# Signs-and-sizes output for one batch half only, whole output weights for the other, and new engine orders

## The reference, cut to what matters

```python
def _tower(x, w_in, b_in, blocks):
    h = _leaky(x @ w_in + b_in)
    for w1, b1, w2, b2 in blocks:
        h = _leaky(_leaky(h @ w1 + b1) @ w2 + b2 + h)
    return h

def step(prev_delta, xk):
    fk, k = xk
    d = where(k == 0, fk[:, 3], prev_delta)
    fk = fk.at[:, 3].set(d)
    fe = _tower(fk[:, :4], fw_in, fb_in, flat_blocks)      # depends on the step before
    pe = _tower(fk[:, 4:], pw_in, pb_in, path_blocks)      # does not
    h = _leaky(concatenate([fe, pe], -1) @ cw1 + cb1)
    delta = sigmoid(h @ cw2 + cb2)[:, 0]
    return delta, delta
```

## Time and profile before

| | us |
|---|---|
| median of 3 runs | 1308.1 (1307.48 to 1308.73) |
| the profiled execution's own time | 1308.0 |
| its span | 1306.2 |
| PE busy | 1284.5 (98%) |
| PE weight loads | 1049.5 (80%) |
| ACT busy | 996.0 (76%) |
| DVE busy | 866.4 (66%) |
| POOL busy | 23.2 (2%) |

### The profile page before, as it was taken

The page is one execution under the profiler, slowest core; times in us unless marked ns, Lnnn a source line. Parts: engine busy times, 40 slices in busy tenths (PEclk is TensorE's granted clock), DMA queues, the critical chain, the costliest instruction groups (busy, mean ns, idle before and its releaser), DMA issues.

```text
span 1306.2 us, 20302 instructions
## 1 busy us (share of the span) xinstructions
PE 1284.5 (98%) x6020; PEld 1049.5 (80%) x6020; DVE 866.4 (66%) x1801; ACT 996.0 (76%) x2177; POOL 23.2 (2%) x19
## 2 busy tenths in 40 slices
PE   5999999999999999999999999999999999999998
PEld 3788888888888888888888888888888888888885
DVE  4676666666666666666766666666676666666665
ACT  1677877777787777777778777777777777777786
POOL 6000000000000000000000000000000000000000
PEclk9999999999999999999999999999999999999999
DMA  4400000000000000000000000000000000000000
GB/s 151 190 10 9 11 11 9 9 12 10 9 11 11 9 11 10 10 9 11 11 9 11 11 9 10 11 10 9 11 10 10 11 10 10 10 11 10 9 7 2
DMA packets 14033, 23.53 MB, mean 18 GB/s; under 512 B 6324, under 2 KB 6760, under 8 KB 13160
## 3 DMA queue, kind: packets, MB, share of 16 engines
q1 hardware_dynamic: 13640, 22.23, 5.4%
q10 hardware_dynamic: 288, 0.01, 0.0%
HBM read 15.66 MB, written 6.55 MB: 17 GB/s over the span
## 4 chain that ended last, share of the span: by engine, by line
PE 97%; DVE 1%; ACT 1%; DMA 1%; issue 0%; SPq 0%; DVEq 0%; ACTq 0%
PE ps_path L438 34%; PE ps_res L441 19%; PE ps_flat L438 17%; PE ps_head L528 8%; PE ps_head L533 8%; PE ps_head L541 4%; PE ps_path L453 2%; PE ps_head L546 2%; PE ps_flat L497 2%; DVE p_res L347 1%; DMA x_lo<-chunk_lo 0%; ACT head L244 0%; DMA chunk_x<-x 0%; ACT head_hi L244 0%; DVE p_sum L350 0%
## 5 line engine op out<-in xcount | busy, mean ns | idle before, releaser
L244 ACT ACTIVATE f_mid<-ps_flat,columns_sb 128x256 f32<-128x256 f32 x512 | 243.0, 475 | 190.3 <-PE ps_flat L438 184.0
L441 PE MATMUL ps_res<-f_mid,hidden_w 128*128 128x256 f32 x1024 | 318.6, 393 | 0.5
L438 PE MATMUL ps_path<-p_mid,hidden_w 128*128 128x256 f32 x1024 | 306.4, 382 | 0.8 <-ACT p_mid L244 0.8
L244 ACT ACTIVATE f_res<-ps_res 128x256 f32<-128x256 f32 x512 | 196.1, 383 | 62.9 <-PE ps_res L441 62.6
L350 DVE SCALAR_TENSOR_TENSOR p_sum<-ps_path,columns_sb,p_res 128x512 f32<-128x512 f32 x128 | 96.0, 750 | 223.0 <-PE ps_path L438 223.0
L441 PEld LDWEIGHTS ps_res<-f_mid,hidden_w 128*128 128x128 f32 x1024 | 164.3, 188 | 82.6 <-ACT f_mid L244 43.2
L438 PEld LDWEIGHTS ps_path<-p_mid,hidden_w 128*128 128x128 f32 x1024 | 196.0, 192 | 28.6 <-ACT p_mid L244 1.5
L407 DVE TENSOR_SCALAR ps_res<-f_res,columns_sb 128x256 f32<-128x256 f32 x256 | 123.6, 483 | 121.0 <-ACT f_res L244 121.0
L347 DVE SCALAR_TENSOR_TENSOR p_res<-p_sum 128x512 f32<-128x512 f32 x256 | 182.3, 712 | 0.1
L244 ACT ACTIVATE p_mid<-ps_path,columns_sb 128x512 f32<-128x512 f32 x256 | 175.1, 684 | 7.7 <-PE ps_path L438 7.7
L528 PE MATMUL ps_head<-p_res,hidden_w 128*128 128x256 f32 x512 | 153.5, 382 | 3.8 <-DVE p_res L347 3.8
(11 more groups left out here) (39 smaller groups left out, 1390.0 us busy)
## 6 DMA issues: line engine op xcount, KB each, us to landing
x_path<-x_hi SPq DMA_DIRECT2D x256, 16.0 KB
x_path<-x_lo SPq DMA_DIRECT2D x256, 16.0 KB
x_flat<-x_hi SPq DMA_DIRECT2D x256, 6.0 KB
x_flat<-x_lo SPq DMA_DIRECT2D x256, 6.0 KB
chunk_x<-x SPq DMA_DIRECT2D x2, 1152.0 KB, 7.2
x_hi<-chunk_hi SPq DMA_DIRECT2D x2, 1152.0 KB, 8.8
x_lo<-chunk_lo SPq DMA_DIRECT2D x2, 1152.0 KB, 11.4
out<-delta SPq DMA_DIRECT2D x128, 2.0 KB
```

The costliest lines, as they stand in the source:

```text
L244: return act.activation(dst, src, ACT.Prelu, bias=bias, scale=scale, alpha=NEG)
L438: return pe.matmul(dst, weight[w_name], src, start=True, stop=True)
L441: return pe.matmul(dst, weight[w_name], src, start=False, stop=True, skip_group_check=True)
```

## The change

1. Group 0 keeps the signs and the two one-pass products. Its sizes now sit in its combine weights: `cw1_scaled` holds cw1 with each column multiplied by |c|, made once at the start. ScalarE then needs no scale for `head`, only the scaled bias. `head_hi` is no longer a second activation, but a copy of `head` to fp32r on VectorE.
2. Group 1 drops signs, sizes, `head_hi` and `head_lo`. Its head is the plain leaky with cb1, and one fp32 matmul with `cw2_rep`, the output weights repeated over 128 columns, makes the output (`output`).
3. The leaky of `path_2b` (p_res2) moves from VectorE to ScalarE.
4. The lists of the three engines are new: group 1 runs half a step apart from group 0, and its `flat_1a` and `flat_1b` of the next step stand at the end of a body.
5. At the start come one more small DMA (cw2 as a row), a small matmul that spreads that row over the partitions, and four VectorE steps that make `cw2_rep`, `cw2_sizes` and `cw1_scaled`. PE now waits for five of these parts instead of two.

```diff
+            cw2_at = COLUMNS.index("cw2")
+            act.dma_start(cw2_row[:, :], w["columns"][:, cw2_at:cw2_at + 1].rearrange("p a -> a p"),
+                          allow_slow_non_contiguous=True)\
+               .then_inc(s_columns, 16)
...
-            def leaky(dst, src, bias=0.0, scale=1.0):
-                return act.activation(dst, src, ACT.Prelu, bias=bias, scale=scale, alpha=NEG)
+            def leaky(dst, src, bias=0.0):
+                return act.activation(dst, src, ACT.Prelu, bias=bias, alpha=NEG)
...
+            def path_2b(k):
+                par = k % 2
+                if exists(k):
+                    act.wait_ge(s_p2b_t, k + 1)
+                    leaky(p_res2[par][:, :], p_sum2[:, :]).then_inc(s_p2b_h, 1)
...
-                    leaky(head[g][:, :], combined(g), cb1_scaled[:, :], cw2_size[:, :]).then_inc(s_head_h[g], 1)
-
-            def head_high(k, g):
-                if exists(k):
-                    act.wait_ge(s_head_mm[g], k + 1)
-                    leaky(head_hi[g][:, :], combined(g), cb1_scaled[:, :], cw2_size[:, :]).then_inc(s_head_hi[g], 1)
+                    leaky(head[g][:, :], combined(g), cb1_scaled[:, :] if g == SPLIT else column["cb1"]).then_inc(s_head_h[g], 1)
...
+            dve.tensor_copy(cw2_rep[:, :], column["cw2"].to_broadcast([HID, HID])).then_inc(s_cw2, 1)
+            dve.wait_ge(s_cw2_rows, 1)
+
+            dve.tensor_copy(cw2_copy[:, :], cw2_rows).then_inc(s_cw2_parts, 1)
+            dve.wait_ge(s_cw2_parts, 3)
+            dve.scalar_tensor_tensor(cw2_sizes[:, :], cw2_copy[:, :], -1.0, cw2_copy[:, :],
+                                     ALU.mult, ALU.max).then_inc(s_cw2_parts, 1)
+            dve.wait_ge(s_cw2_parts, 4)
+            dve.wait_ge(s_w_loaded, 16)
+            for i, n in enumerate(("cw1_flat", "cw1_path")):
+                dve.tensor_tensor(cw1_scaled[:, i * HID:(i + 1) * HID], weight[n], cw2_sizes[:, :],
+                                  ALU.mult).then_inc(s_cw2, 1)
...
+            def head_high(k, g):
+                if exists(k):
+                    dve.wait_ge(s_head_h[g], k + 1)
+                    dve.tensor_copy(head_hi[g][:, :], head[g][:, :]).then_inc(s_head_hi[g], 1)
...
+            def cw1(g, part):
+                if g == SPLIT:
+                    return cw1_scaled[:, part * HID:(part + 1) * HID]
+                return weight[("cw1_flat", "cw1_path")[part]]
...
-                    pe.matmul(combined(g), weight["cw1_path"], cols(p_res2[par], g), start=True, stop=False)
+                    pe.matmul(combined(g), cw1(g, 1), cols(p_res2[par], g), start=True, stop=False)
...
-                    pe.matmul(combined(g), weight["cw1_flat"], f_res2[g][:, :], start=False, stop=True)\
+                    pe.matmul(combined(g), cw1(g, 0), f_res2[g][:, :], start=False, stop=True)\
                       .then_inc(s_head_mm[g], 1)
+
+            def output(k, g):
+                if exists(k):
+                    pe.wait_ge(s_head_h[g], k + 1)
+                    pe.matmul(outcome(g), cw2_rep[:, :], head[g][:, :], start=True, stop=True)\
+                      .then_inc(s_out_mm[g], 1)
...
+                combine_path(k, 0)
+                output(k, 1)
+                combine_flat(k, 0)
...
+            pe.wait_ge(s_one_row, 1)
+            pe.wait_ge(s_columns, 48)
+            pe.matmul(cw2_rows, one_row[:, :], cw2_row[:, :], start=True, stop=True).then_inc(s_cw2_rows, 1)
+            pe.wait_ge(s_cw2, 5)
```

More of the change, by code:

```diff
@@ L198, in _ @@
             sp.wait_ge(s_chunk_stored[0], 32)
[L199 to L200 removed]
+            body(0)
+            body(1)
             for c in range(1, CHUNKS):
@@ L298, in delta_out, with body @@
                                    bias=cb2_col[:, :]).then_inc(s_delta[g], 1)
-            def body(k, par):
+            def body(k):
                 flat_1a(k, 0)
-                flat_1a(k, 1)
+                flat_2a(k, 1)
                 flat_1b(k, 0)
-                flat_1b(k, 1)
+                flat_2b(k, 1)
                 flat_2a(k, 0)
-                flat_2a(k, 1)
+                head_out(k, 1)
                 flat_2b(k, 0)
                 path_in(k + 3)
-                flat_2b(k, 1)
+                delta_out(k, 1)
                 head_out(k, 0)
-                head_high(k, 0)
-                head_out(k, 1)
-                head_high(k, 1)
-                delta_out(k, par, 0)
+                path_2b(k + 1)
                 path_1a(k + 3)
-                delta_out(k, par, 1)
+                delta_out(k, 0)
+                flat_1a(k + 1, 1)
                 path_2a(k + 2)
+                flat_1b(k + 1, 1)
             bodies(act, body)
@@ L370, in path_2b_sum, with flat_delta @@
                     add(p_sum2[:, :], ps_path2[:, :], column["pr2_b2"], p_res1[par][:, :]).then_inc(s_p2b_t, 1)
[L372 to L377 removed]
+            def flat_delta(k, g):
+                par = k % 2
                 if exists(k):
@@ L489, in path_2b, with flat_x @@
                         product(half(ps_path2, h), "pr2_w2", half(p_mid2, h)).then_inc(s_p2b_mm, 1)
-            def flat_x(k, par, g):
+            def flat_x(k, g):
+                par = k % 2
                 if exists(k):
@@ L547, in output_low, with body @@
                       .then_inc(s_out_mm[g], 1)
-            def body(k, par):
+            def body(k):
                 flat_1a(k, 0)
-                combine_path(k, par, 1)
-                flat_1a(k, 1)
-                flat_1b(k, 0)
-                path_1b(k + 2, 1)
-                flat_1b(k, 1)
-                flat_2a(k, 0)
                 path_2b(k + 1, 0)
                 flat_2a(k, 1)
-                flat_2b(k, 0)
-                path_in(k + 3, 1 - par)
+                path_in(k + 3)
+                flat_1b(k, 0)
+                combine_path(k, 1)
                 flat_2b(k, 1)
-                combine_flat(k, 0)
+                flat_2a(k, 0)
                 path_2b(k + 1, 1)
                 combine_flat(k, 1)
-                flat_x(k + 1, 1 - par, 1)
+                flat_x(k + 1, 1)
+                flat_2b(k, 0)
+                combine_path(k, 0)
+                output(k, 1)
+                combine_flat(k, 0)
+                path_2a(k + 2, 0)
                 path_1a(k + 3, 0)
+                path_1a(k + 3, 1)
                 output_high(k, 0)
-                path_1a(k + 3, 1)
+                path_2a(k + 2, 1)
                 output_low(k, 0)
-                flat_x(k + 1, 1 - par, 0)
-                output_high(k, 1)
-                path_2a(k + 2, par, 0)
-                output_low(k, 1)
-                path_2a(k + 2, par, 1)
-                combine_path(k + 1, 1 - par, 0)
+                flat_x(k + 1, 0)
+                flat_1a(k + 1, 1)
                 path_1b(k + 3, 0)
+                path_1b(k + 3, 1)
+                flat_1b(k + 1, 1)
             pe.wait_ge(s_w_loaded, 16)
             pe.wait_ge(s_in_split, 2)
-            pe.wait_ge(s_cw2, 2)
+            pe.wait_ge(s_one_row, 1)
+            pe.wait_ge(s_columns, 48)
+            pe.matmul(cw2_rows, one_row[:, :], cw2_row[:, :], start=True, stop=True).then_inc(s_cw2_rows, 1)
+            pe.wait_ge(s_cw2, 5)
+            pe.wait_ge(s_cw2_parts, 3)
             for g in range(GROUPS):
```

85 lines of the change are left out of this document (46 added, 39 removed).

## The result

| | before | after |
|---|---|---|
| median | 1307.79 us (4 runs, 1307.29 to 1308.73) | 1288.72 us (4 runs, 1286.61 to 1289.41) |
| profiled execution: own time, span | 1308.0, 1306.2 | 1288.14, 1286.3 |
| a step in the steady state | 9.908 | 9.773 |

The ratio of after to before is 0.9851, with a 95% interval of 0.9834 to 0.9868: 1.5% faster. The sign and the bound on the whole were right; what failed are two terms of the sum, the 0.02 us a step charged for handovers and the +1.0 us for the start.

The account below looks back on a forecast made before the run. PE, busy 1250.33 of 1251 us at full clock, was taken to bound the kernel. Steps -13.7, start +1.0 and end -1.3 us summed to -14.0 against 1308.0, giving 1294 us, range 1290 to 1306.

Parts of the forecast that it names:

- The bound: Whole kernel: the sum of what PE runs in a step sets the time, PE being busy 1250.33 of 1251 us.
- (e): Each step: handovers that could not be bounded well, charged 0.02 us a step, bounds 0 and 0.10.
- (f): Start: +1.0 us, bounds -0.5 and +4, with f_in of group 1 meeting GpSimd's subtraction and four matmuls at half clock.
- (a): Output of group 1: two short matmuls go and one fp32 comes, +0.191 us a step, +24 us in 127 steps.
- (b): PE's chain: losses of 0.17 at flat_2b of group 1, 0.12 and 0.02 at output_high go, -0.31 us a step.
- (c): The cast on VectorE, 128x256, SBUF to SBUF: takes 0.33 us, bounds 0.22 and 0.55, with 0.40 allowed.
- (d): ACT and DVE in a step: p_res2 on ACT takes 0.383 to 0.77 us, hidden up to 0.85; DVE is no bound.
- (g): End, from the last flat_1a of group 0 to the last delta's end: 7.60 us instead of 8.87, -1.3 us.
- A: Rival on the steady steps: the margins are not there, 0.06 us a step lost, step 9.85, 1300 us; chance 0.20.
- B: Rival on PE's chain: the losses belong to the one-pass matmuls, step 10.08, +22 us, 1330 us; chance 0.08.
- C: Rival on VectorE: the cast takes 0.551 us as in its start-up row, 0.21 a step lost, 1320 us; chance 0.06.

Follow-up runs that it names:

- experiment 2: The kernel before, in its own orders, with only group 1's output made one fp32 matmul with the whole output weights, head unscaled: 1313.76 us, ratio 1.0039.
- experiment 1: The kernel before with path_in moved ahead of flat_2b of group 0 instead of behind it: 1326.41 us, ratio 1.0136.
- experiment 4: The changed kernel with output_low and flat_x of group 0 swapped on PE: 1299.89 us, ratio 0.9929.
- experiment 8: The changed kernel's own orders with signs and one-pass parts for group 1 too, its cast and subtraction on VectorE: 1340.05 us, ratio 1.0241.
- experiment 3: The changed kernel with one more cast of head of group 0, to a spare tile, ahead of the real one on VectorE: 1307.29 us, ratio 0.9991.
- experiment 6: The changed kernel with the leaky p_res2 put back on VectorE from ScalarE: 1290.67 us, ratio 0.9869.
- experiment 5: The changed kernel itself once more, unaltered, as the level for the next runs: 1288.73 us, ratio 0.9851.
- experiment 9: A new kernel, run beside the kernel before: signs and one-pass parts for both groups, with orders laid out anew for them: 1273.70 us, ratio 0.9739.

## Why the prediction was right, and what it missed

The bound, the losses and the cast came out as told. Two terms of the sum failed: (e), 0.02 us a step for handovers that cost nothing, together with a loss taken for rounding; and (f), +1.0 us for the start, which gained 1.5. Together they put the forecast some 5 us too high.

**The bound, and (a) the swap.** Right. PE is full before and after, every gain and loss is a slot of its chain, and group 1's new output costs what was said: +0.194 by slots averaged over 100 steps, for +0.191, and in experiment 2 the step grew by 0.059 where this price met the 0.13 of waits that it took away.

**(b) The losses.** Right, and shown as waits for ScalarE, not as a property of the array, for the 0.17 (experiment 1). For the 0.12 the prices add up: with the load at 610.00, 0.27 to the slot and 0.12 for it, `output_high` of group 1 ends at 610.39, where the chain has its end. All of them went. The spare of 0.03 in group 0's recurrence held (experiment 4). Experiment 8 shows the other side: with signs for group 1 too, the same orders cost 0.39 a step.

The list of checks lacked one. `output_high` of group 0 waits for the same cast, and with the cast's end at 609.97, 0.12 to the load and 0.27 to the slot it could start at 610.36, 0.07 before its turn at 610.43. Experiment 3 agrees: a cast 0.21 later cost it 0.13. So this matmul, and not `flat_1a` of group 1 as the prediction has it, sets the limit on the cast: 0.295 + 0.08, about 0.37, instead of 0.40. The cast stayed under both.

**(c) The cast.** Taken as 0.33 with bounds 0.22 and 0.55; it took 0.295. The Trainium skill's arithmetic (VectorE: DVE Perf Modes, "Side-by-side": two elements a cycle and about 150 cycles fixed) gave 0.30, and the trace agrees with it. The estimates were not all worked out alike, though: 0.30 and 0.43 take in the section's 8 cycles of pipe fill and 0.22 does not, which with them is 0.23. Of my rows the 384-column one, run in the start-up, was too slow to interpolate from.

**(d) ScalarE and VectorE.** Right: p_res2 took 0.62 there, hidden, and moving it back leaves the step at 9.773 (experiment 6).

**(e) and the step.** The first term that failed, in size alone. I charged 0.02 a step for handovers, and no wait came. And of the 0.02 that I called rounding, half was a loss: the losses of the kernel before, averaged over 100 steps, are 0.168, 0.124, 0.028 and, not on my list, 0.009 in the slot right behind `output_high` of group 1. They make 0.33 and not 0.31. In the chain of before this slot is 0.44:

```profile
610.39 0.44 PE ps_path L438 x2
```

The other half was the price of the fp32 slot, 0.4317 and not 0.431. The sum took off 0.31 and 0.01. The step fell by 0.135 and not 0.108, which is 3.4 us in 127 steps: more than half of the miss. The late handover of the cast that I feared is there (its end 609.97, the subtraction's start 610.08, 0.11) against 0.04 in the sum; the shorter cast paid for half of it.

**(f) The start.** The second term that failed: +1.0 forecast (37.9 - 36.1 - 0.8, with no place left for the +0.3 of the new steps ahead), -1.5 measured (the first `flat_1a` of group 0 begins in its slot at 34.67, against 36.14, with about the same stretch of slow clock behind it). I had f_in of group 1 meet GpSimd's subtraction, and the clock halved for the four matmuls behind it. In the profiled execution neither held. VectorE, GpSimd and PE there:

```profile
27.99 1.16 DVE L373 SCALAR_TENSOR_TENSOR f_in<-f_t 128x256 f32<-128x256 f32 x1
28.95 5.11 POOL L241 TENSOR_TENSOR chunk_lo<-chunk_x,chunk_hi 128x2304 fp32r<-128x2304 f32 x1
...
30.42 3.92 DVE L373 SCALAR_TENSOR_TENSOR f_in<-f_t 128x256 f32<-128x256 f32 x1
...
34.40 0.70 PE L466 MATMUL ps_flat<-f_in,hidden_w 128*128 128x256 f32 x2 [2.81 <-DVE f_in L373]
```

f_in of group 1 slipped in ahead, its four matmuls ran at full clock, and only f_in of group 0 waited. In the execution of experiment 5 f_in of group 1 was caught (29.96, 3.95 us long), as I had priced it, but the clock stayed at 1.00, and the first `flat_1a` of group 0 came at 35.95, not 37.9. So the term was wrong in both: it took the slow clock for these four matmuls as given, and had the full clock only as one end of its bounds (-0.5). The new steps at the start (five on VectorE, not four) cost less than the +0.3: the first `path_in` record is at 11.24 against 11.11.

**(g) The end.** -1.3 forecast, -1.0 measured: 1276.87 to 1284.74 is 7.87 us, 0.27 over the 7.60, because I added pure handovers where other matmuls of the list stand between two stages for longer.

```profile
1276.71 0.59 PE L466 MATMUL ps_flat<-f_in,hidden_w 128*128 128x256 f32 x2
...
1284.27 0.47 ACT L313 ACTIVATE delta<-ps_head,cb_col 128x256 f32<-128x256 f32 x1 [1.33 <-PE ps_head L590]
```

Together: -17.1 (steps) - 1.5 - 1.0 = -19.6, against 19.9 between the spans. The forecast of -14.0 missed 3.4 in the steps and 2.5 at the start, and erred by 0.3 the other way at the end. The range failed with them. Its low end was worked out as 1288.7 (no loss at all in the steps, the start at -0.5, the end at -1.3) and then raised to 1290, because all three at once seemed unlikely. The steps came out so, the start better than its bound and the end a little worse, and the median is 1288.72.

**The rivals.** A (margins not there) did not come about; experiments 3 and 4 show how near it was. B fell in experiments 1 and 2. C fell with the cast's 0.295.

Left open: no run took the 0.12 at `output_high` of group 1 away and kept the rest, so that it was head_hi's rests on the sum above; and which part of the start's gain belongs to which edit is known for p_res2 alone (1.9 us, experiment 6).

## What to carry to other kernels

When one in-order engine is full, price each handover once from the trace (end of one record to start of the next) and lay out a new order as slots: the waits then come out to 0.01 or 0.02 us, at worst to 0.05 (experiment 3), and cheaper work in the wrong place can lose to dearer work in the right one (experiments 8 and 9). Lay out the lists of the other engines too: in experiment 8 one late delta held up the next cast on two of them at once. A few hundredths that don't add up in a step of a long loop can be a real loss (here half of them were); find them before choosing a range. And look at the start separately: here cutting the long instructions of a helper engine gained 5 us, a quarter of what the whole change gained.

## What the runs showed of the hardware that I had not expected

**Which of VectorE and GpSimd goes first differs from run to run.** The same program, at 18.6 us, in the profiled execution of the changed kernel and in that of experiment 5 (VectorE and GpSimd):

```profile
18.57 0.69 DVE L373 SCALAR_TENSOR_TENSOR p_res<-p_sum 128x512 f32<-128x512 f32 x1
18.64 2.58 POOL L239 CAST chunk_hi<-chunk_x 128x2304 fp32r<-128x2304 f32 x1
```

```profile
18.55 2.11 POOL L240 CAST chunk_hi<-chunk_x 128x2304 fp32r<-128x2304 f32 x1
18.65 2.55 DVE L374 SCALAR_TENSOR_TENSOR p_res<-p_sum 128x512 f32<-128x512 f32 x1
```

Whoever starts later is drawn out by about what the other still has to run. The profiled executions of the two differ by 1.1 us in span.

**The slow clock after a pause is not sure either.** After 2.81 us of idle PE the granted clock was 0.50 over 36 to 39 us in one execution of the changed kernel; after 2.19 us it stayed at 1.00 in the other, which had the slow stretch in the last steps instead (0.61 over 1277 to 1280).

**The slow handover of head_hi is not one of every rounded tile.** PE and VectorE (609.97 to 610.08) start 0.11 after its writer's record ends, where other handovers take 0.04 or 0.05. But head_lo is a tile of fp32r too, and it is read after 0.05. Both in one chain, in the last step of the changed kernel:

```profile
1282.97 0.30 DVE head_hi L437
...
1283.30 0.02 DVEq L442
...
1283.36 0.44 DVE head_lo L443
...
1283.85 0.40 PE ps_head L590
```

The readers of head_hi wait for two semaphores, head's first and head_hi's second (L441 and L442, L583 and L584), and the chain shows the second wait as an instruction of its own, L442, between the cast and the subtraction. The reader of head_lo has one wait. At the start of the same run f_t of group 0, whose second wait is for `flat_x` (L408), starts 0.11 after that matmul ends, and its input is no fp32r tile. So the second wait is the likelier cause; no run swaps or drops it.
